# A conditional product written as two 64-row matmuls per chunk instead of one 128-row matmul against a block-diagonal operand

## What is computed

```python
def _L0_cond_ref(x, condition, weights):          # x (64, 64, 1024), weights (16, 64, 64)
    W = weights[condition]
    return jnp.einsum('bct,bcd->bdt', x, W)

def _L0_ffn_ref(x, A, B, Wr):                     # 4096 rows of 1024; A, B: 64 experts of rank 16
    scores = xf @ Wr.T
    top_vals, top_idx = jax.lax.top_k(scores, 16)
    gates = jax.nn.softmax(top_vals, axis=-1)
    G = jnp.zeros((N, K), xf.dtype).at[jnp.arange(N)[:, None], top_idx].set(gates)
    h = jnp.einsum('nd,krd->nkr', xf, A)
    out = jnp.einsum('nkr,kdr->nd', h * G[:, :, None], B)
    return (out * 2.0).reshape(*prefix, -1)

x = x + _L0_ffn_ref(_L0_cond_ref(x, itok_B_0_15, L0_cond_weights), L0_ffn_A, L0_ffn_B, L0_ffn_Wr)
```

## Time and profile before

| | before |
|---|---|
| median of 3 runs | 738.26 us (736.23 to 739.06) |
| profiled execution, whole time | 737.22 us |
| profiled execution, span from first to last instruction | 735.4 us |
| PE busy | 716.5 us, 97% of the span |
| PE weight loads (PEld) busy | 600.9 us, 82% |
| DVE busy | 490.9 us, 67% |
| ACT busy | 262.8 us, 36% |
| mean granted TensorE clock | 0.995 of full speed |

### The profile page before, as it was taken

The page is one execution under the profiler, slowest core; times in us unless marked ns, Lnnn a source line. Parts: engine busy times, 40 slices in busy tenths (PEclk is TensorE's granted clock), DMA queues, the critical chain, the costliest instruction groups (busy, mean ns, idle before and its releaser), DMA issues.

```text
span 735.4 us, 9259 instructions
## 1 busy us (share of the span) xinstructions
PE 716.5 (97%) x3440; PEld 600.9 (82%) x3440; DVE 490.9 (67%) x945; ACT 262.8 (36%) x498; POOL 51.4 (7%) x38
## 2 busy tenths in 40 slices
PE   8999989789999999999999999999999999999998
PEld 7878777578888888888888888888888888888886
DVE  4598899997433867965435469885544386887742
ACT  4567663332532642122222443312222264223100
POOL 0694700000000000000000000000000000000000
PEclk9999999899999999999999999999999999999999
DMA  9958349556986775566668586747577767544663
GB/s 321 408 202 289 121 166 404 210 209 261 310 309 227 285 261 203 210 215 235 238 245 289 200 324 236 246 162 270 199 256 256 270 249 290 185 170 175 228 227 143
DMA packets 56158, 178.41 MB, mean 243 GB/s; under 512 B 9650, under 2 KB 9778, under 8 KB 55602
## 3 DMA queue, kind: packets, MB, share of 16 engines
q1 hardware_dynamic: 53954, 172.78, 64.8%
q10 hardware_dynamic: 2160, 5.05, 1.9%
HBM read 131.66 MB, written 46.14 MB: 242 GB/s over the span
## 4 chain that ended last, share of the span: by engine, by line
PE 85%; DVE 13%; DMA 1%; issue 1%; ACT 0%; POOL 0%; DVEq 0%; POOLq 0%
PE Pb L265 38%; PE Pb L247 35%; PE Cb L227 6%; PE S L281 4%; DVE Cq L363 3%; DVE Wt L198 3%; DVE Op L180 2%; DMA xc<-in_x 1%; PE T L509 1%; DVE R L363 1%; DVE Xo L180 1%; DVE BR L363 1%; DVE xc L363 1%; DVE Q L363 1%; PE T L298 0%
## 5 line engine op out<-in xcount | busy, mean ns | idle before, releaser
L247 PE MATMUL Pb<-Op,Wt 128*128 128x512 f32 x1008 | 239.2, 393 | 6.4 <-DVE Op L180 4.6
L247 PEld LDWEIGHTS Pb<-Op,Wt 128*128 128x128 f32 x1008 | 187.4, 188 | 46.2 <-DVE Op L180 6.3
L265 PE MATMUL Pb<-Wt,Op 128*128 128x512 f32 x912 | 214.8, 394 | 7.0 <-DVE Op L180 7.0
L265 PEld LDWEIGHTS Pb<-Wt,Op 128*128 128x128 f32 x912 | 171.3, 190 | 43.5 <-DVE Op L180 8.7
L363 DVE TENSOR_TENSOR Q<-Pb,Q 128x512 f32<-128x512 f32 x112 | 77.4, 691 | 88.3 <-PE Pb L265 88.3
L265 PE MATMUL Pb<-Wt,Ox 128*128 128x512 f32 x432 | 100.8, 391 | 0.0
L265 PEld LDWEIGHTS Pb<-Wt,Ox 128*128 128x128 f32 x432 | 80.6, 188 | 16.3
L233 ACT COPY R<-Cb 128x512 f32<-128x512 f32 x60 | 35.2, 586 | 161.7 <-PE Cb L227 161.7
L180 DVE TENSOR_TENSOR Op<-R,Op 128x512 fp32r<-128x512 f32 x94 | 68.5, 753 | 28.8 <-ACT Op L178 28.8
L363 DVE TENSOR_TENSOR Cq<-Pb,Cq 128x512 f32<-128x512 f32 x64 | 44.0, 687 | 40.9 <-ACT Cq L374 30.9
L247 PE MATMUL Pb<-Ox,Wt 128*128 128x512 f32 x288 | 66.3, 390 | 0.0
(11 more groups left out here) (89 smaller groups left out, 486.9 us busy)
## 6 DMA issues: line engine op xcount, KB each, us to landing
Wt<-Wd SPq DMA_DIRECT2D x168, 512.0 KB, 4.9
Wd<-Wt SPq DMA_DIRECT2D x56, 512.0 KB, 4.2
Q<-in_x SPq DMA_DIRECT2D x32, 512.0 KB, 5.0
xc<-in_x SPq DMA_DIRECT2D x24, 512.0 KB, 4.0
out<-Q SPq DMA_DIRECT2D x32, 256.0 KB, 2.5
out<-Q SPq DMA_DIRECT2D x16, 512.0 KB, 2.8
BR<-in_x SPq DMA_DIRECT2D x12, 256.0 KB, 10.1
BR<-in_B SPq DMA_DIRECT2D x3, 1024.0 KB, 7.9
```

Of the source, the lines that this page charges most:

```text
L247: t = pe.run(lambda e, c=c, o=o, a=a, z=z: e.matmul(Pb[:, b, :], Wt[:, k, a, 128 * c:128 * c + 128], part(o, z), start=fresh and (c, a, z) ...
L265: t = pe.run(lambda e, c=c, o=o, k=k, a=a, z=z: e.matmul(Pb[:, b, :], part(o, a)[:, 128 * i:128 * i + 128], Wt[:, k, z, :], start=fresh an ...
```

## The change

The zero blocks of the moving operand go, and with them the memset. `wbd` shrinks to 64 columns for each tile: rows 0 to 63 hold the matrix of the first batch, rows 64 to 127 that of the second. Each chunk becomes two matmuls, one on rows 0 to 63 and one on rows 64 to 127 of the same chunk of x, with 128 stationary and 64 moving columns each. The two write to two different PSUM banks (`to[:, h, ...]`), and two halves of a tile now share both banks: a pair of halves fills columns 0 to 255 and 256 to 511 of both. `cond_pair` therefore waits for both banks, makes all its matmuls, and then both copies to `R` follow, each reading both banks. `S` and `T` become the two banks of one tensor `ST`. The four products ahead of everything take `Cb` and `ST` in turn, and the third and fourth wait until DVE has split the first and second. Core of the diff:

```diff
-        wbd = sb("wbd", [128, 8, 128], F32)
+        wbd = sb("wbd", [128, 8, 64], F32)
...
-        S = pb("S", [128, 512])
-        T = pb("T", [128, 4, 128])
+        ST = pb("ST", [128, 2, 512])
+        S, T = ST[:, 0, :], ST[:, 1, :].rearrange("p (a n) -> p a n", n=128)
...
+        def cond_part(to, at, src, i, a):
             for c in range(4):
+                for h in range(2):
+                    t = pe.run(lambda e, c=c, h=h: e.matmul(
+                        to[:, h, at + 64 * c:at + 64 * c + 64],
+                        src[64 * h:64 * h + 64, 512 * a + 128 * c:512 * a + 128 * c + 128],
+                        wbd[64 * h:64 * h + 64, i, :], start=True, stop=True), (c, h) == (3, 1))
+            wbd_free[i] = t
+            return t
+
+        def by_batch(whole):
+            return whole.rearrange("p c (h d) -> p h c d", d=64)
+
+        def cond_pair(halves, *tokens):
+            pe.after(cb_free[0][0], cb_free[1][0], *tokens)
+            for k, (src, i, a) in enumerate(halves):
+                pe.after(wbd_ready[i])
+                t = cond_part(Cb, 256 * k, src, i, a)
             ac.after(t, R_free[0])
+            for k, (src, i, a) in enumerate(halves):
+                to = by_batch(R[:, i // 4, 4 * a:4 * a + 4, 128 * (i % 4):128 * (i % 4) + 128])
+                cb_free[0][0] = cb_free[1][0] = R_ready[i // 4][a] = ac.run(lambda e, k=k, to=to: e.copy(
+                    to, Cb[:, :, 256 * k:256 * k + 256].rearrange("p h (c d) -> p h c d", d=64)))
...
-        z_w = gp.run(lambda e: e.memset(wbd[:, :, :], 0.0))
...
         for i in range(4):
-            pe.after(wbd_ready[i], x0_ready[i][1])
...
+            to, at = (Cb, ST)[i % 2], 256 * (i // 2)
+            pe.after(wbd_ready[i], x0_ready[i][1], parts[i - 2] if i > 1 else None)
+            t = cond_part(to, at, x0[i], i, 1)
...
-                        for a in (1, 0):
-                            t = cond_half(xc[:, k % 2, :], k, a, xc_ready[k % 2])
-                        xc_free[k % 2] = t
+                        xc_free[k % 2] = cond_pair([(xc[:, k % 2, :], k, a) for a in (1, 0)], xc_ready[k % 2])
```

More of the change, by code:

```diff
@@ L219, in a_source @@
                     Q[:, j + 4, 0:512], Q[:, j + 4, 512:1024])[m]
[L221 to L225, removed]
+        def cond_part(to, at, src, i, a):
             for c in range(4):
[L227 to L230, removed]
+                for h in range(2):
[12 more added lines that the diff above has]
+                t = cond_part(Cb, 256 * k, src, i, a)
             ac.after(t, R_free[0])
-            cb_free[b][0] = R_ready[i // 4][a] = ac.run(
-                lambda e: e.copy(to, Cb[:, b, :].rearrange("p (c n) -> p c n", n=128)))
-            wbd_free[i] = t
+            for k, (src, i, a) in enumerate(halves):
+                to = by_batch(R[:, i // 4, 4 * a:4 * a + 4, 128 * (i % 4):128 * (i % 4) + 128])
+                cb_free[0][0] = cb_free[1][0] = R_ready[i // 4][a] = ac.run(lambda e, k=k, to=to: e.copy(
+                    to, Cb[:, :, 256 * k:256 * k + 256].rearrange("p h (c d) -> p h c d", d=64)))
             return t
@@ L424, in cond_weights @@
                 i, h = 4 * half + b // 2, b % 2
-                sp.after(wbd_free[i], z_w)
+                sp.after(wbd_free[i])
                 wbd_ready[i] = sp.load(l_w[i], lambda e, b=b, i=i, h=h: e.dma_start(
-                    wbd[64 * h:64 * h + 64, i, 64 * h:64 * h + 64],
+                    wbd[64 * h:64 * h + 64, i, :],
                     wts[64 * h:64 * h + 64, bass.ds(which[b], 1), :].rearrange("c a d -> c (a d)")))
@@ L513, in a_unit @@
             made[m, j] = unit(4 * m + j, a_source(m, j), *tokens, free=free, bank=bank)
-        cond_first(0, cn, t_wa, z_w)
-        banks = [Cb[:, 0, :], Cb[:, 1, :], S[:, :], T[:, :, :].rearrange("p a n -> p (a n)")]
+        cond_first(0, cn, t_wa)
         turns, parts = [], []
         for i in range(4):
-            pe.after(wbd_ready[i], x0_ready[i][1])
[L521 to L525, removed]
+            to, at = (Cb, ST)[i % 2], 256 * (i // 2)
+            pe.after(wbd_ready[i], x0_ready[i][1], parts[i - 2] if i > 1 else None)
+            t = cond_part(to, at, x0[i], i, 1)
             turns.append(t)
-            whole = banks[i].rearrange("p (c n) -> p c n", n=128)
-            up, low = [Op[:, 0:4, a, 128 * i:128 * i + 128] for a in range(2)]
+            whole = to[:, :, at:at + 256].rearrange("p h (c d) -> p h c d", d=64)
+            up, low = [by_batch(Op[:, 0:4, a, 128 * i:128 * i + 128]) for a in range(2)]
             ac.after(t)
@@ L538, in adaln_ffn @@
         for i in range(4):
[L539 to L542, removed]
+            to, at = (Cb, ST)[i % 2], 256 * (i // 2)
+            ac.after(parts[2 + i % 2])
+            R_ready[0][1] = ac.run(lambda e, i=i, to=to, at=at: e.copy(
+                by_batch(R[:, 0, 4:8, 128 * i:128 * i + 128]),
+                to[:, :, at:at + 256].rearrange("p h (c d) -> p h c d", d=64)))
+            for free in ((cb_free[0], cb_free[1]), (s_free, t_free))[i % 2]:
+                free[0] = R_ready[0][1]
             if i < 2:
@@ L704, in adaln_ffn @@
                     if s == 0:
[L705 to L708, removed]
+                        pair = {(0, 0): ((0, 0), (1, 0)), (0, 1): ((2, 0), (3, 0)), (0, 2): ((4, 0), (5, 0)),
+                                (0, 3): ((6, 0), (7, 0)), (1, 0): ((4, 1), (5, 1)), (1, 1): ((6, 1), (7, 1))}
+                        if (m, j) in pair:
+                            cond_pair([(x0[i], i, a) for i, a in pair[m, j]], *[x0_ready[i][a] for i, a in pair[m, j]])
                         if (m, j) == (0, 3):
```

## The result

The changed kernel takes 749.3 us (748.34 to 750.15, 4 runs) against 738.3: a ratio of 1.0155, 95% interval 1.0136 to 1.0174. It is slower, as forecast, but by 11 us and not by 52. The profiled execution took 748.79 us, its span 747.0.

The account below looks back on a forecast made before the run. PE's own stream was taken to bound the kernel. Terms 42.7 + 7.1 + 3.2 + 0.6 - 1.1 = 52.5 us, on the profiled 737.2, gave 790 us (chance 0.50), own range 778 to 803; the range from 738 to 803 also took in rival A.

Parts of the forecast that it names:

- What bounds the kernel, and what binds a pair: PE's stream sets the time; in a conditional-product pair, loads and streaming balance at 0.111 us per load with matmul.
- The doubled loads: Conditional-product pairs: 32 loads one after the other, +1.78 us a pair; 42.7 us in slices 1 to 3, 7.1 in slice 0.
- changes of mode: Going from whole array to halves and back at each pair: taken as nothing, bounds 0 to 9 us.
- the distance between loads: Sign in a pair of the changed kernel: 0.11 us if the forecast is right, 0.055 in rival A.
- rival A: Loads of the two halves overlap, a pair stays at 1.78 us: 739 to 748 us, middle 742; chance 0.31.
- Rival B: Halves overlap and a 64-row load takes half the time, a pair takes 0.89 us: 714 us; chance 0.11.
- Rival C: Nothing overlaps in a pair, loads and matmuls in turn, 5.3 us a pair: about 841 us; chance 0.08.
- The start: Four products ahead of everything: +3.2 us with doubled loads, +1.1 us from the new waits if products kept 0.89 us.
- The copies: Both copies to `R` follow a pair's last matmul: second ends 0.6 us later, +0.6 us once through `sum_t1`.
- The wait for `xc`: Last pair of slice 0: PE's 1.1 us wait for a transfer vanishes under longer pairs, -1.1 us.
- The early pairs: Six pairs in slice 0: first four delay the chain by 7.1 us, last two's 3.6 us hidden beside DVE work.

Follow-up runs that it names:

- streams with 32 moving columns: Matmuls on zeros put behind the warm-up of the kernel before, 32 moving columns each: both halves of the array took 2.80 us, whole array 1.48 us.
- the quarters: Each chunk as four matmuls on array quarters with 64 stationary columns: on zeros 1.56 us for 24 rounds; as an edit of the changed kernel 726.44 us, 0.9858.
- the stream of four and four: Matmuls on zeros behind the warm-up of the kernel before, four of one array half, then four of the other; the other half's first started at 36.11 us.
- quarters and no new wait: Changed kernel with matmuls on array quarters, four pairs of banks at the start, two pairs at one place in slices 1 and 2: 724.74 us, 0.9841.

## Why the prediction was right and wrong

*What bounds the kernel, and what binds a pair: right.* PE's stream is the chain, and the load of 128 stationary columns, 0.11 us, binds it; the streaming that the change halves was hidden. The streams with 32 moving columns and the quarters show both. "Slower" was forecast and came true, but in part by luck: the term that made nearly all of it is nothing, and what made the kernel slower is a term put at nothing and the loss at the start.

*The doubled loads: wrong, and this is the step that failed.* I took the larger end of 0 to +1.78 us for a pair, loads one after the other, and it was the smaller: +0 in the stream. The argument was that a load begins when the matmul before it begins, and that a load for the other half would have to overtake a matmul that hasn't begun. The first half is what rows of whole-array matmuls show, and they can show nothing else, since there all loads want the same rows. The second half of the argument doesn't hold: in the stream of four and four, the other half's matmuls start ahead of earlier ones of the first. Of the sum's 52.5 us, 42.7 + 7.1 stood on this; measured were 0.36 for each of 30 pairs, 10.8 us, all from the changes of mode, less the 2.9 that slice 0 covers. The sign named for this, the distance between loads, came out as rival A's: (1.86 - 0.19)/31 = 0.054 us, not 0.11. (The lower end of the range that went with this forecast, 778, should be 779 by its own terms.)

*The changes of mode: wrong at nothing.* I named the bound, 0.16 us each and 9 us in all, and took zero. Measured: 0.34 us for both ways in the stream alone, 0.36 in the kernel, 8.6 us for the 24 pairs of `xc`. The reason that I gave for zero, that changes between kinds of matmul in the trace are free, was about data types on the whole array, another thing. The Trainium skill's rule (TensorEngine Tiling (Array Packing), Key Properties) is that a change of mode drains TensorE. The trace agrees in size: 0.15 us going and 0.19 coming back, near the 0.16 of a matmul's hidden part. The draining itself is in no row.

*Rival A* had the rule that loads and matmuls of different row groups run at once (the Trainium skill, TensorE: Matmul & The Clock Gate, Part 3). The traces agree: 32 loads in 1.86 us. With mode changes at their bound it gave 748; measured 749.3. It had a chance of 0.31 and should have had the larger one. The same part of that page says that matmuls start and end strictly in the order of the program; across the two halves the stream of four and four doesn't do that: a matmul of the second half started at 36.11 and ended by the profile at 36.43, ahead of the start of the first half's last one, 36.44.

*Rival B* had the right mechanism for a gain with the wrong measure: a load gets shorter with its columns, not with its rows. *Rival C* fell.

*The start: right in kind, missed in size.* For unchanged products I had +1.1 us for the waits; the last split ended 16.84 instead of 14.65, +2.2, and the step behind it took 1.46 us more. What was missing is the clock: PE idled 1.2 us at the new wait, and the granted clock fell to its lower level soon after. The last split was later in part for the same reason, and in part because the third product began at 12.50 and not at the 11.88 of the prediction: the first row of the start's chain, the load of ACT's table (L536), ended at 11.03, in the kernel before at 10.54. For the doubled loads I had put +3.2 us, near the +3.65 measured, by luck: the cause named is absent.

*The copies* put `sum_t1` 0.5 us further behind its pair, where 0.6 was put, and a copy that reads two banks takes 590 ns, before 587. But the sum had `sum_t1` in the chain, and it no longer is, so this term is nothing in the total. *The wait for `xc`*: -1.3, where -1.1 was put, but it was used up by the changes of mode, not by longer streams; it is gone without the late start too. *The early pairs*: four were put on the chain and two beside it at nothing. All six stand in it, and 1.6 us of PE's waits for DVE covered some of them and of the start's loss.

## What to carry to other kernels

When two sides of an instruction stream are in balance, find which of them a rewrite shrinks and which it doesn't: the small matmuls here were bound by the load of the stationary columns, so cutting rows and moving columns gave nothing and cutting stationary columns gave 0.84 us a pair. A switch between whole-array and tiled matmuls cost about a third of a microsecond there and back here, so tiled work should stand together or be large at each place. And a new short wait on TensorE early in a kernel is to be priced with the clock, not by its own length alone: 1.2 us of waiting came with 3.65 us lost.

## What was not expected of the hardware

- Two 64-row halves ran side by side with 0.111 us for a load and matmul in each, the same as one half alone (2.82 us for 24 rounds in both).
- The four quarters took 0.06 us a round (1.56 us for 24), four fp32 loads and matmuls of 64x64 in about half the time of one on the whole array.
- A wait of 1.2 us on PE, soon after the warm-up, was followed by a stretch at the lower clock (0.72 of full speed over 12 us); the same kernel without the wait kept the full clock there. This was seen in both directions: with the waits added to the kernel before it was 0.86, with them taken from the changed one 1.00. The wait needn't be for a semaphore of this kind: with quarters and no new wait PE idled 2.5 us at one stretch ahead of the first step, and the clock fell as well, while a single stretch of 1.8 us there in the kernel before left it full.
